# Halving the row-sum matmuls of an attention kernel, and reordering its first two groups

## The reference

```python
xn = layernorm(x)
# attention: a compressed state of 64 numbers per token
c = xn @ W_to_kv.T @ W_compress.T
ch = layernorm(c) * gamma + beta
q = rope(ch @ Wq.T); k, v = split(ch @ Wkv.T); k = rope(k)
p = softmax(where(causal, q @ k.T / 8, -1e30))
z = (p @ v) @ W_comp2lat.T
attn = z @ W_to_kv + z @ W_out_res.T + b_out
# experts: 16, each 512 -> 256 -> 512, the best 2 per token
logits = xn @ router.T
shared = (silu(xn @ Sg) * (xn @ Su)) @ Sd
out = x + attn + shared + sum over the token's 2 experts of w_e * expert_e(xn)
```

## Time and profile before

| | |
|---|---|
| median of 3 runs | 1832.99 us (1831.64 to 1833.00) |
| the profiled execution | 1835.32 us, its span 1833.5 us |
| PE busy | 1755.7 us, 96% of the span |
| DVE busy | 1130.7 us, 62% |
| ACT busy | 771.8 us, 42% |
| POOL busy | 662.4 us, 36% |
| granted PE clock, mean | 0.985 |

### The profile page before, as it was taken

One profiled execution on the slowest core, in us unless ns is written; L12 is line 12 of the kernel. 1 busy time (PEld: TensorE's weight loads), 2 busy tenths in 40 slices (PEclk: granted clock), 3 DMA queues, 4 the chain that ended last, 5 costly groups with the idle time before them and its releaser, 6 DMA issues. The chain is left out here.

```text
span 1833.5 us, 28152 instructions
## 1 busy us (share of the span) xinstructions
PE 1755.7 (96%) x8477; PEld 1402.1 (76%) x8477; DVE 1130.7 (62%) x2227; ACT 771.8 (42%) x1319; POOL 662.4 (36%) x676
## 2 busy tenths in 40 slices
PE   5699999999999998999999999999999989999998
PEld 3587778787877786778788877778888867777776
DVE  7777667777766653455555555555555436766676
ACT  3232332233222322333333344333333368888885
POOL 2544544545444442343434333433334321011110
PEclk9799999999999999999999999999999999999999
DMA  7667777766677665644544545555445438899896
GB/s 247 244 199 236 219 218 221 240 205 192 206 231 215 200 183 192 198 136 157 184 170 166 177 166 194 178 180 172 165 164 185 153 75 188 205 239 197 208 223 163
DMA packets 149934, 352.52 MB, mean 192 GB/s; under 512 B 20476, under 2 KB 41916, under 8 KB 149824
## 3 DMA queue, kind: packets, MB, share of 16 engines
q1 hardware_dynamic: 97276, 234.52, 39.5%
q0 software_dynamic: 43968, 104.91, 22.5%
q10 hardware_dynamic: 8580, 11.64, 2.3%
HBM read 208.24 MB, written 146.70 MB: 194 GB/s over the span
## 5 line engine op out<-in xcount | busy, mean ns | idle before, releaser
L1486 POOL DMA_INDIRECT expert_rows<-res,ids_all x143 | 150.1, 1050 | 444.8 <-ACT res L1308 435.9
L1427 DVE TENSOR_REDUCE mx<-emb 128x1 f32<-128x512 f32 (+3 forms) x288 | 175.1, 641 | 106.7 <-PE emb L1227 85.2
L70 PE MATMUL egu<-w,rT_0h 128*128 x576 | 186.9, 406 | 1.1 <-DVE rT_0l L1398 1.1
L70 PE MATMUL egu<-w,rT_1h 128*128 x568 | 182.5, 402 | 0.0
L1404 DVE TENSOR_TENSOR eh<-egu,esg 128x256 f32<-128x256 f32 x143 | 60.7, 424 | 183.6 <-ACT esg L1298 183.5
L1682 ACT ACTIVATE ex<-sc 128x1024 f32<-128x1024 f32 (+4 forms) x176 | 144.8, 823 | 55.1 <-PE sc L1627 47.3
L1034 POOL DMA_INDIRECT token_list<-tok,slot x128 | 127.1, 993 | 112.9 <-DVE slot L741 77.0
L1481 POOL DMA_INDIRECT rows<-xn_scratch,rows_all x137 | 132.9, 970 | 48.3 <-issue 43.1
L1298 ACT ACTIVATE esg<-egu 128x256 f32<-128x256 f32 x143 | 55.0, 384 | 204.7 <-PE egu L70 202.0
L1747 POOL DMA_DIRECT2D base<-expert_rows x32 | 41.3, 1527 | 264.8 <-DMA base<-base_scratch 244.2
L996 POOL TENSOR_TENSOR xb<-x,bias 128x512 f32<-128x512 f32 x64 | 88.7, 1417 | 87.9 <-DVE h_l L765 87.9
(11 more groups left out here) (283 smaller groups left out, 4563.7 us busy)
## 6 DMA issues: line engine op xcount, KB each, us to landing
w<-expert_parts SPq DMA_DIRECT2D x64, 768.0 KB, 8.5
base<-expert_rows POOLq DMA_DIRECT2D x32, 1024.0 KB, 12.5
expert_parts<-ew_h SPq DMA_DIRECT2D x32, 768.0 KB
expert_parts<-ew_l SPq DMA_DIRECT2D x32, 768.0 KB
x<-x SPq DMA_DIRECT2D x16, 1024.0 KB, 6.2
xn_scratch<-xn SPq DMA_DIRECT2D x16, 1024.0 KB, 8.5
base_scratch<-xb SPq DMA_DIRECT2D x16, 1024.0 KB, 12.2
base<-base_scratch SPq DMA_DIRECT2D x16, 1024.0 KB, 6.5
```

What stands on the lines that cost most here:

```text
L70: mm = pe.matmul(dst, w, m, start=(first and i == 0), stop=(last and i == len(terms) - 1))
L1427: dve.tensor_reduce(mx[n % 2][:, j, c:c + 1], mb[g % 2][:, 0:width], AX.X, ALU.max).then_inc(m_red, 1)
L1486: pool.indirect_dma_start(parts_d[:, :], bass.IndirectOffsetOnAxis(ap=ids_all[:, t:t + 1], axis=0), res[t % 2][:, :], None, bounds_check=2 ...
```

## The change

Row sums: the column of ones moves from 63 to 32 (`ONE`). The rows 64 to 127 of `oT` belong to the values' low halves, and row 96 (64 + 32) among them holds nothing that is needed. DVE writes the row sum's low part into row 96 of the high half, after `output_low`, and `last` has a one in rows 32 and 96. So one matmul per block gives the sum. `fold` is changed so that row 96 doesn't enter the projection. `project_at` begins one step later. `vs` is copied in two pieces around the column of ones.

The first groups: the constants have two semaphores, the first four loads count on `first_consts`. ACT issues the loads of the three matrices. `sh_gate` goes to another borrowed place (`gate_in`), and x(1) is issued right behind the constants. ACT's casts of `sh_gate` and `sh_up` go in between the blocks of group 0. `zeros` is now made by POOL in `xb4[1]`, after the second matrix's low half, and the list is cleared after the normed rows of group 1 are stored. Group 1's sums, norm and blocks come earlier in all lists. Of the expert quarters only (0, 0) stays in `first_step`; (0, 1), (1, 0) and (1, 1) are in `second_step`, the last two behind blocks of group 2. SP's two steps are written out.

```diff
@@ -54,7 +54,7 @@
 EH = EW // 2
-CA = C + 1
+ONE = C // 2
...
@@ -163,8 +163,9 @@
 cs = [placed(f"cs_{i}", [P, 2, GROUP], F32, 8 * EH + 2 * i * GROUP) for i in range(2)]
-zeros = value(xT[1][1][:, :, :]).rearrange("p k t -> p (k t)")[:, 0:2 * LIST // P // 3]
 h = [sb(f"h_{c}", [P, FC, GROUP], F32R) for c in "hl"]
+zeros = xb4[1][:, :, :].rearrange("p j d -> p (j d)")[:, 0:2 * LIST // P // 3]
+gate_in = placed("gate_in", [P, KD, FS], F32, 0)
 ht = sb("ht", [P, GROUP])
...
@@ -282,17 +283,47 @@
         load_x(0, 0)
+        for dst, src in first_loads:
+            sp.dma_start(dst, src).then_inc(first_consts, 16)
         for dst, src in loads:
             sp.dma_start(dst, src).then_inc(consts, 16)
-        for i, (dst, src) in enumerate(zip(staged, (sh_gate, sh_up, sh_down))):
-            sp.dma_start(dst, src.rearrange("(k p) f -> p k f", p=P)).then_inc(weights_in[i], 16)
         load_x(1, 1)
+        load_cs(0, 0)
+        load_ew(0, 0)
         store_xn(0)
-        load_ew(0, 0)
-        sp.wait_ge(setup, 1)
+
+    def clear_list():
+
+        sp.wait_ge(blank, 2)
         for part in range(3):
             sp.dma_start(list_d.rearrange("(a p c) o -> a p (c o)", a=3, p=P)[part], zeros.bitcast(I32)).then_inc(cleared, 16)
-        load_cs(0, 0)
+
+    def store_base(s, q):
+        sp.wait_ge(d_ev, 4 * s + 4)
+        hold(sp, sp_gate)
+        sp.dma_start(pick_g(base_g, s), xb4[q][:, :, :]).then_inc(st_base[q], 16)
+
+    def first_step():
+        load_cs(1, 1)
+        store_xn(1)
+        clear_list()
+        store_ew(0, 0)
+        load_ew(0, 1)
+        store_qkv(0, 0)
+        load_x(2, 0)
+        store_ew(0, 1)
+        load_ew(1, 0)
+
+    def second_step():
+        load_cs(2, 0)
+        store_xn(2)
+        load_x(3, 1)
+        store_ew(1, 0)
+        load_ew(1, 1)
+        store_qkv(1, 1)
+        store_base(0, 0)
+        store_ew(1, 1)
+        load_ew(2, 0)
...
@@ -373,10 +406,10 @@
             pe.wait_ge(t_ev, 4 * s + 4)
-            if known(s, 0):
-                pe.wait_ge(split_done, 2)
         g, u = gb[2 * (f % 2)], gb[2 * (f % 2) + 1]
-        for dst, w in ((g, wgp), (u, wup)):
+        for i, (dst, w) in enumerate(((g, wgp), (u, wup))):
+            if known(s, 0) and f == 0:
+                pe.wait_ge(split_done, i + 1)
             mm = parts(pe, dst[:, :], [([a[:, k, f * P:(f + 1) * P] for a in w], [a[:, k, :] for a in xT[q]])
...
@@ -475,10 +508,10 @@
     def second_step():
+        logits(1, 1)
         shared_gu(0, 0, 2)
-        logits(1, 1)
+        logits_back(1)
         shared_gu(0, 0, 3)
-        logits_back(1)
         shared_down(0, 0, (0, FC - 1))
...
@@ -542,12 +575,23 @@
         act.wait_ge(ew_in, 96 * n + 48 * c + 48)
+        if known(n, 0) and c == 0:
+            act.wait_ge(split_done, 1)
         after(act, ew_st, 64 * n + 32 * c)
...
     def first():
-        for j in range(GT):
-            turned(0, 0, j)
+        act.wait_ge(first_consts, FIRST_CONSTS)
+        for i, (dst, src) in enumerate(zip(staged, (sh_gate, sh_up, sh_down))):
+            act.dma_start(dst, src.rearrange("(k p) f -> p k f", p=P)).then_inc(weights_in[i], 16)
+        act.wait_ge(setup, 1)
+        act.activation(sg[0][:, 0:1], sg[0][:, 0:1], ACT.Silu)
+        weights_high(0)
+        turned(0, 0, 0)
+        turned(0, 0, 1)
+        weights_high(1)
+        turned(0, 0, 2)
+        turned(0, 0, 3)
...
@@ -577,31 +620,32 @@
     def first_step():
-        weights_high()
         logits_out(0)
+        weights_high(2)
         expert_high(0, 0)
         silu(0, 0)
-        hidden_high(0, 0)
         state_high(0)
         silu(0, 1)
+        hidden_high(0, 0)
+        swapped(0)
+        for j in range(GT):
+            turned(1, 1, j)
         hidden_high(0, 1)
-        expert_high(0, 1)
-        swapped(0)
-        for j in range(GT):
-            turned(1, 1, j)
     def second_step():
+        logits_out(1)
         silu(0, 2)
         hidden_high(0, 2)
-        logits_out(1)
-        expert_high(1, 0)
+        expert_high(0, 1)
         silu(0, 3)
...
         state_high(1)
+        swapped(1)
+        for j in range(GT):
+            turned(2, 0, j)
+            if j == 1:
+                expert_high(1, 0)
         expert_high(1, 1)
-        swapped(1)
-        for j in range(GT):
-            turned(2, 0, j)
...
@@ -784,18 +827,14 @@
         dve.memset(ones[:, :], 1.0)
-        dve.memset(zeros, 0.0).then_inc(blank, 1)
-        dve.wait_ge(blank, 1)
-        dve.memset(zeros.bitcast(I32).rearrange("p (c o) -> p c o", o=2)[:, :, 0], 2 * N)
+        dve.memset(sg[0][:, 0:1], 0.0)
         for i, number in enumerate((-0.5, -1.0, math.e)):
             dve.memset(powers[:, i, :], number)
-        dve.memset(vs[0][:, :, C - 1:C], 1.0)
-        dve.memset(vs[1][:, :, C - 1:C], 1.0).then_inc(setup, 1)
+        dve.memset(vs[0][:, :, ONE:ONE + 1], 1.0)
+        dve.memset(vs[1][:, :, ONE:ONE + 1], 1.0).then_inc(setup, 1)
         norm_sums(0, 0)
         norm(0, 0)
-        dve.wait_ge(consts, CONSTS)
-        dve.tensor_copy(before[:, :], tri[:, 0, :])
-        dve.tensor_copy(carry[:, :], rt[:, GT, :])
+        dve.wait_ge(first_consts, FIRST_CONSTS)
         dve.wait_ge(wc_done, 1)
...
@@ -867,45 +910,42 @@
     def first_step():
-        weights_low(0)
         weights_low(1)
...
         normed(0)
-        weights_low(2)
         norm_sums(1, 1)
-        hidden(0, 0)
-        hidden_low(0, 0)
         scaled(0)
         state_low(0)
+        norm(1, 1)
+        hidden(0, 0)
+        roped(0, 0)
+        for j in range(GT):
+            turned_low(1, 1, j)
+            if j == 0:
+                roped_swapped(0, 0)
+                hidden_low(0, 0)
         expert_low(0, 0)
-        norm(1, 1)
         hidden(0, 1)
+        weights_low(2)
         hidden_low(0, 1)
-        roped(0, 0)
-        expert_low(0, 1)
-        roped_swapped(0, 0)
-        for j in range(GT):
-            turned_low(1, 1, j)
-            if j == 1:
-                slots(0, 0)
+        slots(0, 0)
...
         hidden(0, 2)
+        compressed(1)
         hidden_low(0, 2)
-        norm_sums(2, 0)
-        expert_low(1, 0)
-        hidden(0, 3)
-        hidden_low(0, 3)
-        compressed(1)
         choose(1)
...
         normed(1)
+        expert_low(0, 1)
+        hidden(0, 3)
+        norm_sums(2, 0)
+        hidden_low(0, 3)
         norm(2, 0)
...
         state_low(1)
-        expert_low(1, 1)
         for j in range(GT):
...
@@ -915,6 +955,8 @@
                 slots(1, 1)
+                expert_low(1, 0)
+        expert_low(1, 1)
...
@@ -990,6 +1032,7 @@
             pool.wait_ge(split_done, 3)
+            pool.wait_ge(xn_done, 2)
         after(pool, st_base[q], times(n, q))
...
@@ -1018,11 +1061,17 @@
             return
-        if not known(n, NG - 1) and not known(n, 0):
+        early = known(n, 0) or known(n, 1)
+        if not known(n, NG - 1) and not early:
             root(n + 1, 0, mvx, rsx, mvx_done, rsx_done)
...
         if known(n, 0):
-            root(1, 0, mvx, rsx, mvx_done, rsx_done)
+            pool.wait_ge(split_done, 2)
+            pool.memset(zeros, 0.0).then_inc(blank, 1)
+            pool.wait_ge(blank, 1)
+            pool.memset(zeros.bitcast(I32).rearrange("p (c o) -> p c o", o=2)[:, :, 0], 2 * N).then_inc(blank, 1)
+        if early:
+            root(n + 1, 0, mvx, rsx, mvx_done, rsx_done)
         weighted(n, q)
...
@@ -1562,7 +1611,7 @@
     for j in range(GT):
-        free = max(free, final[k] + LAG + 2)
+        free = max(free, final[k] + LAG + 3)
         project_at[free] = (k, j)
...
@@ -1649,9 +1698,7 @@
             for i in range(GT):
-                for c in range(2):
-                    mm = pe.matmul(ob[k % 2][:, 2 * i:2 * i + 2], oT[k % 2][c][:, i * P:(i + 1) * P], last[:, :],
-                                   start=(c == 0), stop=(c == 1))
+                mm = pe.matmul(ob[k % 2][:, 2 * i:2 * i + 2], oT[k % 2][0][:, i * P:(i + 1) * P], last[:, :], start=True, stop=True)
             mm.then_inc(l_done, 1)
...
@@ -1710,7 +1757,10 @@
         dve.wait_ge(o_hi, k + 1)
-        dve.tensor_tensor(oT[k % 2][1][:, :], ob[k % 2][:, :], value(oT[k % 2][0][:, :]), ALU.subtract).then_inc(o_ev, 1)
+        dve.tensor_tensor(oT[k % 2][1][:, :], ob[k % 2][:, :], value(oT[k % 2][0][:, :]), ALU.subtract).then_inc(o_low, 1)
+        dve.wait_ge(o_low, k + 1)
+        dve.tensor_tensor(oT[k % 2][0][C + ONE:C + ONE + 1, :], ob[k % 2][ONE:ONE + 1, :], value(oT[k % 2][0][ONE:ONE + 1, :]),
+                          ALU.subtract).then_inc(o_ev, 1)
...
@@ -1724,8 +1774,10 @@
-    dve.tensor_copy(last[:, :], ident[:, C - 1:C + 1]).then_inc(ready, 1)
-    dve.memset(value(qlm[2][C:P, :]), 0.0).then_inc(blank, 1)
+    dve.memset(value(qlm[2][C:P, :]), 0.0)
+    for i in range(2):
+        one = dve.tensor_tensor(last[:, i:i + 1], ident[:, ONE:ONE + 1], ident[:, C + ONE:C + ONE + 1], ALU.add)
+    one.then_inc(ready, 1)
     for i in range(TAIL):
```

70 lines of the change are left out of this document (37 added, 33 removed).

## The result

The changed kernel takes 1839.05 us (median, 1836.27 to 1844.17), the kernel before, run beside it, 1833.64 us. The ratio is 1.0028 (95% interval 1.002 to 1.0037): about 5 us slower, where 1.7 us faster was forecast, and outside the range that was given, by 0.55 us. (The kernel before itself came out 0.65 us above the 1832.99 from which the forecast was counted, so that the range was missed is a close call; the direction and the size are not.) The profiled execution took 1843.53 us with a span of 1841.7 us, against 1835.32 and 1833.5. It is one of the slower executions of the changed kernel, so its trace shows a larger loss at the end (8.2 us) than the medians do.

A forecast was written before the change was run, and what follows sets the result against it. It took TensorE, busy nearly throughout from 98.35 us on, as the bound. The start's +7.3 us and the row sums' -9.0 us gave -1.7 us, so 1832.99 becomes 1831.3 us, range 1821.5 to 1838.5.

The forecast's parts named there:

- Part 1: Attention stage: four row-sum matmuls per group instead of eight, issued one step later; -9.0 us, bounds -11 and +1.4.
- a step of later issue covers the first four: 2.9 us gained: Attention stage: issuing row sums a step later hides TensorE's waits for the output's low half in four groups; 2.9 us gained.
- (d): Attention stage: the added subtraction delays DVE's products for PE in all groups, 10.4 us, total 1841; chance 0.09 shared with (e).
- (e): Attention stage: four row-sum matmuls take what eight took, total 1838.5; chance 0.09 shared with (d).
- Part 2: Start up to group 0's rows: weight loads issued by ACT share engines with SP; group 0 ready at 25.2 instead of 20.55.
- rival (b): Start: ACT's loads aren't slowed by SP's; group 0 ready at 21.5, everything behind 3.7 us earlier, total 1827.6; chance 0.16.
- the prediction's step from turns to halves: Start: engines switch rings by packet, so ACT's and SP's loads share in halves; the sum grows by 1.6 us.
- Part 3: Group 1's rows: qkv(0) follows without a wait, blocks ready at 52.8 instead of 62.4; 9.6 us won here.
- Part 4: Before qkv(1): GpSimd's bias adds and list writes delay group 1's root; qkv(1) at 85.4 instead of 87.29.
- Part 5: First regular step: expert refills through one staging buffer stall the fourth gate-and-up pair; +7.3 us, bounds -2 and +16.
- I take 9.5: First regular step: each expert refill, from the store's issue to the start of the next cast, takes 9.5 us.
- rival (c): First regular step: both refills cost 14.1 us each, like one with a load of x ahead; total 1840.5; chance 0.12.

The follow-up runs named there:

- later_step_only: The kernel before with one number changed: row sums and projections of each group one step later; ratio 1.0012 to the kernel before.
- start_only: The changed kernel with the row-sum change undone, so only the first groups are reordered; ratio 1.0055 to the kernel before, 10.1 us slower.
- pair_before_logits: The changed kernel with three expert quarters cast one place earlier and group 0's third gate/up pair ahead of group 1's logits; ratio 0.9961 to the kernel before.
- rows_only: The kernel before with the row-sum change alone, first two groups as before; ratio 0.9978 to the kernel before, 4.0 us faster.
- quarters_earlier: The changed kernel with three expert quarters cast one place earlier, SP's stores and refills moved to match; ratio 0.9962 to the kernel before.
- rows_early: The kernel before with the row-sum change alone, but row sums at their old place, one step earlier; ratio 0.9989 to the kernel before.

## Why the prediction was wrong, point by point

**Part 1, the row sums, -9.0 forecast, -4.0 measured (-6.4 to -1.8).** The 7.2 us of matmuls are right: the changed kernel's four take from 1544.22 to 1544.58, the 0.36 us of the working. The tail's 0.7 is right, and so is the 0.65 us for the added subtraction (0.69); `ready` cost 0.7, not 0.4. The step that failed is "a step of later issue covers the first four: 2.9 us gained". The cover is there, but the time came back: the scores' waits for ACT grew by 3.3 us (5.8 to 9.1), and 1.0 us of small waits is new. With waits of 12.2 against 10.1 us the sum is -7.2 + 2.1 + 0.7 = -4.4. `later_step_only` shows the same exchange without the subtraction. The prediction asked who waits for the row sums, and not what the next step's scores wait for once PE comes to them sooner. Rivals (d) and (e) were both wrong.

**Part 2.** Group 0's product came at 22.75, not 25.2, since `sh_up` took 10.7 us from its issue at 8.23, not 13.3. Beside SP's transfers that is 1.2 us more than it took before; in six other traces with the same two queues it was 9.6 to 9.9, so they cost next to nothing, as rival (b) had it. What (b) expected of it, 3.7 us less at the end, didn't come: in `start_only`, too, the refills hold the fourth pair. In the changed kernel `sh_up` landed 4.3 us behind `sh_gate`, from 14.6 to 18.9. In that time the profile counts 532 packets and 1.06 MB on ACT's queue and 533 packets and 0.52 MB on SP's: two thirds of the bytes for the weights and not half. The Trainium skill ("DMA: Bandwidth & Descriptors", section on queues, rings and completion order) says that an engine switches between rings by packet. The trace agrees, with 532 and 533 packets in the same time. What failed is the prediction's step from turns to halves, which gave 26.8: ACT's packets were twice as large as SP's. On one queue, with the loads issued 4.3 us earlier, the product starts at 19.21.

**Part 3.** Right: no wait ahead of qkv(0) (41.69), group 1's blocks ready at 50.6 against 52.8, the difference being mostly part 2's. What was missed is the 6.9 us that PE then waits for `carry`. Taking it away in `pair_before_logits` moved no later milestone forward, though another wait stood there then.

**Part 4.** Right in its mechanism: bias adds at 55.25 (57.3 forecast), last list write ended at 70.9 (72.6), the root directly behind it, qkv(1) at 84.16 (85.4). DVE's choice ended together with the root (72.6 and 72.3), so GpSimd wasn't alone in holding it, and DVE didn't wait for the root as the prediction had it.

**Part 5, +7.3 forecast, +10.1 measured (+7.2 to +12.8).** The mechanism is right and the size of one term is off, the "I take 9.5" for a refill. The third quarter ended at 94.5 (95.6 forecast), ACT waited for `ew` twice as described, PE waited 6.1 us at the fourth pair (7 forecast), and from there to qkv(2) it took 12.9 us (12.8 forecast). The refills were put at 9.5 us each and took 12.9 and 9.7. This is 3.6 us more, the early third quarter takes 1.1 back, and PE reaches the pair at 126.30 instead of 123.5. The earlier trace rows had a warning: the refill of 14.1 us. The prediction named it as rival (c), for both refills, and took the shorter two. The measured pair lies between, one long and one short. Rival (c) put the length down to the load of x ahead; moving that load away gained 1.1 us on the first refill and lost 0.8 on the second. What also sets the three rows apart is GpSimd: list writes run beside the one of 14.1 us (138.83 to 148.83) and not beside the ones of 8.45 and 10.65. If the list writes are the reason, the first refill of the chain was the long one to expect, and the second a short one, as it came. The two misses, 5.0 us in part 1 and 2.8 in part 5, add to 7.8 us against the 6.8 between forecast (-1.7) and result (+5.1); either part as forecast would have left the result inside the range.

**What stays open.** Between the first gathered expert rows (706.27 and 714.94) and the first scores the changed kernel lost another 2.4 us. In `rows_only` and `start_only` that stretch took 789.6 and 788.4 us, against 788.3 before and 790.7 after, and 790.6 in `quarters_earlier`. So it varies by 1 to 2 us with the same code there. No run tells why.

The first stage varies more. From qkv(2) to qkv(14) the kernel before took 449.5 us, `later_step_only`, with the same code up to the attention stage, 455.4, `rows_only` 444.6 and the changed kernel 447.6. The attention stage of `start_only` took 343.6 us with the code that took 338.9 before. So a difference between two single traces far from the place that was changed says little below some 5 us, in the first stage below 10, and it is the medians that carry the sizes of the two halves. The first 130 us agree better: without the reordered start qkv(2) is at 128.85 to 129.87 in five traces, and with it at 137.12 in `start_only` and 139.24 in the changed kernel.

## What to carry to other kernels

With one staging buffer, the work can go no faster than the chain of cast, store and refill, and each cast moved later moves all refills behind it. Price each refill by one of the trace that has the same transfers beside it, those of the other queues too: here the two took 12.9 and 9.7 us. A wait that is removed ahead of one instruction of TensorE is only a gain if the next thing that it needs is already there; ask for the next wait of the same engine. Reordering the shared queue moved the sum of two refills by 0.3 us here, and only casting each quarter earlier removed the loss.

## What the hardware showed that was not expected

Waits of TensorE of only 0.8 to 1.6 us were followed by a drop of the granted clock in the midst of busy stretches. In the kernel before, PE idled 1.56 us ahead of qkv at 252.04; windows of 4 us around it, columns as in the earlier trace rows:

```profile
248.00:252.00 4.00, 2.48 (x11) 1.68 (x9) 3.77 (x4) 1.93 (x4) 0.00 (x0) 1.00 0.01 5
252.00:256.00 4.00, 3.96 (x12) 2.85 (x13) 2.52 (x4) 1.75 (x3) 3.09 (x3) 0.64 0.00 0
256.00:260.00 4.00, 4.00 (x22) 3.37 (x21) 3.96 (x6) 0.59 (x1) 1.97 (x2) 0.93 0.11 18
```

The 0.36 and 0.07 that are missing of 4 us each are 1.7 us, as much as the wait itself. The trace after has 1.00 from 250 to 266 us. Its delay falls from 6.7 us at that qkv (258.72 against 252.04) to 5.8 at the next (299.60 against 293.83), but it is back at 8.4 by qkv(14), so this place alone explains little of how the delay wanders. In `rows_early` a wait of 1.37 us ahead of row sums (1642.13) is followed by 0.82 and 0.75; in `start_only` one of 0.8 us is followed by 0.88 and 0.70 (1780 to 1788), while `rows_only`, with waits of up to 1.1 us in the same stage, has 1.00 in every such window from 1496 to 1816 us. So a short stall was at times followed by a loss of its own size, and which of them is differs from trace to trace of nearly the same code. No run shows that the stall is what lowers the clock. (1.00 is 2.4 GHz, 0.5 the lower level, 1.2 GHz.)
